# Attention outputs turned on TensorE before they are divided, in place of a way through memory, with the batch ends given a later place in the order

## The reference

```
x = x + 0.5 * ffn0(layernorm(x))       # 128 -> 512 -> 512 -> 512 -> 128, SiLU gate, two GELU layers
x = x + attn0(layernorm(x))            # linear attention, no softmax
x = x + 0.5 * ffn0(layernorm(x))
x = x + 0.5 * moe(layernorm(x))        # each batch picks 2 of 8 low-rank experts by its first position
x = x + attn1(layernorm(x))            # 16 heads of 8, rotary, causal softmax, output projection W_O
x = x + 0.5 * moe(layernorm(x))
```

```
attn = softmax(where(causal, q @ k.T * scale, -inf))     # 256 x 256
out  = attn @ v                                          # 256 x 8
y    = concat over heads(out) @ W_O.T                    # 256 x 128
```

## Time and profile before

| | |
|---|---|
| median of three runs | 768.81 us |
| lowest and highest | 764.74, 771.10 us |
| the profiled execution, whole | 767.41 us |
| its span from first to last instruction | 763.1 us |
| TensorE busy | 684.7 us, 90% |
| VectorE busy | 525.3 us, 69% |
| ScalarE busy | 502.8 us, 66% |
| GpSimd busy | 311.1 us, 41% |

### The profile page before, as it was taken

The page is one execution under the profiler, slowest core; times in us unless marked ns, Lnnn a source line. Parts: engine busy times, 40 slices in busy tenths (PEclk is TensorE's granted clock), DMA queues, the critical chain, the costliest instruction groups (busy, mean ns, idle before and its releaser), DMA issues.

```text
span 763.1 us, 14946 instructions
## 1 busy us (share of the span) xinstructions
PE 684.7 (90%) x5660; PEld 500.7 (66%) x5660; DVE 525.3 (69%) x1306; ACT 502.8 (66%) x830; POOL 311.1 (41%) x433
## 2 busy tenths in 40 slices
PE   2889999999999999999999989798879798889886
PEld 1667777778777777777787766555446355555565
DVE  3745455777657655678677768988699785979543
ACT  2767687977788867979777953346645556557541
POOL 2201121133413130224263475646668474545543
PEclk9889999999999999999999999999989898999999
DMA  9100000000110000000011123215534344332111
GB/s 294 46 1 1 0 1 1 1 0 2 38 46 0 1 1 1 0 2 1 26 58 43 43 87 107 85 47 180 169 122 149 132 152 156 102 132 99 66 57 29
DMA packets 47088, 47.29 MB, mean 62 GB/s; under 512 B 3240, under 2 KB 41128, under 8 KB 46760
## 3 DMA queue, kind: packets, MB, share of 16 engines
q1 hardware_dynamic: 47016, 46.33, 18.4%
HBM read 23.51 MB, written 22.54 MB: 60 GB/s over the span
## 4 chain that ended last, share of the span: by engine, by line
PE 47%; DVE 23%; ACT 12%; issue 6%; DMA 6%; SPq 3%; POOL 2%; POOLq 1%; DVEq 0%; ACTq 0%
PE PSA L787 16%; PE PSA L791 15%; DVE MX L1094 8%; DMA LC<-do 4%; DVE LC L1115 3%; ACT PSA L1146 3%; DVE G L1017 2%; PE PSA L804 2%; SPq L1340 2%; PE PSA L959 2%; ACT G L1142 2%; DVE RA L1087 1%; PE PSA L900 1%; ACT ah L1153 1%; ACT L1142 1%
## 5 line engine op out<-in xcount | busy, mean ns | idle before, releaser
L1240 POOL TENSOR_TENSOR RS<-VE,MHALF 128x4 f32<-128x4 f32 x48 | 49.3, 1028 | 229.7 <-DVE VE L999 229.5
L787 PE MATMUL PSA<-ah,WH 128*128 128x512 f32 x320 | 131.3, 410 | 5.7 <-DVE al L1022 3.0
L1094 DVE TENSOR_REDUCE MX<-PSA 128x6 f32<-128x768 f32 x128 | 116.9, 943 | 13.8 <-PE PSA L922 13.7
L791 PE MATMUL PSA<-al,WH 128*128 128x512 f32 x320 | 125.4, 392 | 0.0
L1146 ACT ACTIVATE PSA<-PSA,SC 128x512 f32<-128x512 f32 x128 | 84.7, 661 | 57.4 <-PE PSA L791 56.7
L1222 ACT ACTIVATE PB<-PSA 128x768 f32<-128x768 f32 x128 | 99.2, 820 | 18.3 <-PE PSA L946 18.1
L787 PE MATMUL PSA<-bh,WH 128*128 128x512 f32 x256 | 105.7, 413 | 4.0 <-DVE bl L1022 2.5
L791 PE MATMUL PSA<-bl,WH 128*128 128x512 f32 x256 | 101.2, 395 | 0.0
L1288 POOL TENSOR_SCALAR_AFFINE_SELECT PB<-PB 128x512 f32<-128x512 f32 x128 | 79.7, 636 | 43.1 <-ACT PB L1222 41.7
L1022 DVE TENSOR_TENSOR al<-PSA,ah 128x512 fp32r<-128x512 f32 x64 | 44.2, 691 | 68.8 <-ACT ah L1153 68.8
L787 PEld LDWEIGHTS PSA<-ah,WH 128*128 128x128 f32 x320 | 60.2, 188 | 22.0 <-DVE al L1022 5.2
(11 more groups left out here) (122 smaller groups left out, 1411.1 us busy)
## 6 DMA issues: line engine op xcount, KB each, us to landing
do<-OT SPq DMA_DIRECT2D x15, 512.0 KB, 6.7
KS<-dk SPq DMA_DIRECT2D x32, 192.0 KB
QS<-dq SPq DMA_DIRECT2D x32, 192.0 KB
dk<-CB SPq DMA_DIRECT2D x16, 192.0 KB, 2.3
dq<-CB SPq DMA_DIRECT2D x16, 192.0 KB, 2.4
X<-in_x SPq DMA_DIRECT2D x8, 256.0 KB, 6.9
dk<-CB SPq DMA_DIRECT2D x16, 128.0 KB, 2.2
dq<-CB SPq DMA_DIRECT2D x16, 128.0 KB, 2.4
```

Source lines behind the costliest of these rows:

```text
L787: e.matmul(o, WH[:, col:col + 128], hi, start=first, stop=False)
L791: return e.matmul(o, WH[:, col:col + 128], low, start=False, stop=last)
L1094: e.tensor_reduce(MX[:, u % 2, :, :].rearrange("p t (l g) -> p l t g", l=2)[:, :, :, g], PSA[:, b:b + 2, 0:384].rearrange("p l (t k) -> p ...
L1240: e.tensor_tensor(RS[:, i, :], VE[:, i, :], MHALF[:, :], ALU.pow).then_inc(g_rs, 1)
```

## The change

1. `ot_out`, `vl_in`, `recip`, `norm_out`, `spread` and `sel` are gone, with the memory tensor `do` and the tiles LC and SEL. Every batch, 15 too, ends in the same way.
2. `upright`, two for each batch (h = 0, 1: half of the queries): TensorE turns the four 128x128 blocks of OT for these queries into one bank, so that queries are on partitions and (head, row) on the free side; VectorE takes the reciprocal of the sixteen sums of each query (128x16, from PSUM) into RC, and multiplies the outputs by it into VQ (128x128, with the reciprocal repeated over eight).
3. `flat`, one for each batch: TensorE turns both halves of VQ back, ScalarE copies the bank to VC. Then `proj` as before; W_O is given in its plain order of rows.
4. The planner's priorities and costs: batch ends 6.6 in place of 5 (the last of all jobs), `maxima` 5.2 in place of 3.5, LEAD 28 in place of 14, QUEUED 1.0 in place of 1.5, and longer costs for `peak`, a late `stat`, and the DMAs of `reloc` and `max_out`. A `weigh` of group 0 waits in the plan until the `upright` of two batches before has been laid.

```diff
-    "rest1": [...], "reloc": [("S", 2.95, 2.95), ("D", 3.6)],
+    "rest1": [...], "reloc": [("S", 2.95, 2.95), ("D", 5.0)],
-    "pass1": [...], "peak": [("V", 0.88, 1.0)],
+    "pass1": [...], "peak": [("V", 1.7, 1.8)],
-QUEUED = 1.5
-LEAD = 14
+QUEUED = 1.0
+LEAD = 28
...
-        self.add(3.5, self.maxima(u, p1))
+        self.add(5.2, self.maxima(u, p1))
...
-        self.add(5, self.fin(u, self.last_weigh))
+        self.add(6.6, self.fin(u, self.last_weigh))
...
     def weigh(self, u, g):
+        while self.otfree[u % 2] is None:
+            yield
         b, free = yield from self.sr.get(self)
         w = self.put("weigh", u=u, g=g, b=b, emptied=free, emptied2=self.otfree[u % 2])
+        self.otfree[u % 2] = [] if g < 3 else None
...
     def fin(self, u, w):
         yield from self.until(w.done)
-        if u < NB - 1:
-            o = self.put("ot_out", u=u, c=u // 2, src=w)
-            self.otfree[u % 2] = [o]
+        while self.vqfree is None:
+            yield
+        out, vqfree, self.vqfree = [], self.vqfree, None
+        for h in range(2):
+            b, free = yield from self.sr.get(self)
+            o = self.put("upright", u=u, h=h, b=b, emptied=free, emptied2=vqfree, src=w)
+            self.sr.free[b] = [o]
+            out.append(o)
+        self.otfree[u % 2] = [o]
         while self.vcfree[u % 2] is None:
             yield
-        if u < NB - 1:
-            yield from self.until(o.done - 0.5)
-            ld = self.put("vl_in", u=u, src=o, emptied=self.vcfree[u % 2])
-            self.vcfree[u % 2] = None
-            yield from self.until(ld.done)
-            rc = self.put("recip", u=u, src=ld)
-            on = self.put("norm_out", u=u, src=rc)
-        else:
-            b, free = yield from self.sr.get(self)
-            on = self.put("spread", u=u, b=b, src=w, emptied=free, emptied2=self.vcfree[u % 2])
-            self.sr.free[b] = [on]
+        yield from self.until(o.done)
+        b, free = yield from self.sr.get(self)
+        on = self.put("flat", u=u, b=b, emptied=free, emptied2=self.vcfree[u % 2], src=o)
+        self.vqfree = self.sr.free[b] = [on]
+        self.vcfree[u % 2] = None
         yield from self.until(on.done)
         b, free = yield from self.sr.get(self)
         o = self.put("proj", c=u // 2, u=u, b=b, emptied=free, src=on)
...
# TensorE
+                elif st.name == "upright":
                     w.wait_ge(a_ot, st.src.n + 1)
+                    w.wait_ge(s_w[0], 32)
+                    emptied(w, st.emptied)
+                    for q in range(4):
+                        t = e.transpose(PSA[:, b, 128 * q:128 * q + 128], OT[u % 2][:, q, 128 * st.h:128 * st.h + 128],
+                                        IDN[:, :])
+                    t.then_inc(p_up_right, 1)
+                elif st.name == "flat":
+                    w.wait_ge(v_vq, st.src.n + 1)
+                    emptied(w, st.emptied)
+                    for h in range(2):
+                        t = e.transpose(PSA[:, b, 128 * h:128 * h + 128], VQ[:, h, :], IDN[:, :])
+                    t.then_inc(p_flat, 1)
...
# VectorE
+                elif st.name == "upright":
+                    O = bank(b).rearrange("p (m r) -> p m r", r=32)
+                    w.wait_ge(p_up_right, n + 1)
+                    e.reciprocal(RC[:, st.h, :], O[:, :, 8]).then_inc(v_rc, 1)
+                    w.wait_ge(v_rc, n + 1)
+                    for s in st.emptied2:
+                        w.wait_ge(p_flat, s.n + 1)
+                    e.tensor_tensor(VQ[:, st.h, :].rearrange("p (m r) -> p m r", r=8), O[:, :, 0:8],
+                                    RC[:, st.h, :].rearrange("p (m o) -> p m o", o=1).to_broadcast([128, NH, 8]),
+                                    ALU.mult).then_inc(v_vq, 1)
...
# ScalarE
+                elif st.name == "flat":
+                    w.wait_ge(p_flat, n + 1)
+                    for s in st.emptied2:
+                        w.wait_ge(p_proj, s.n + 1)
+                    e.activation(VC[:, u % 2, :], PSA[:, b, 0:256], ACT.Copy).then_inc(a_vc, 1)
```

More of the change, by code:

```diff
@@ L157, in put @@
         t = ready
-        for i, (eng, us, *way) in enumerate(TAKES[name]):
+        late = name + "_late" if self.dead and name + "_late" in TAKES else name
+        for i, (eng, us, *way) in enumerate(TAKES[late]):
             if eng == "D":
@@ L672, in build @@
         s_m = [sem(f"s_m{u}") for u in range(KEPT)]
-        s_dv = [sem(f"s_dv{u}") for u in range(2)]
-        s_vl = [sem(f"s_vl{u}") for u in range(2)]
-        s_out, s_sel, p_spread, v_on = sem("s_out"), sem("s_sel"), sem("p_spread"), sem("v_on")
+        s_out, p_up_right, p_flat, v_vq, a_vc = (sem(n) for n in ("s_out", "p_up_right", "p_flat", "v_vq", "a_vc"))
         p_xtf, p_up, p_hid, p_down, p_back = (sem(n) for n in ("p_xtf", "p_up", "p_hid", "p_down", "p_back"))
```

63 lines of the change are left out of this document (12 added, 51 removed), and 14 rows, old and new, of the table TAKES.

## The result

The changed kernel takes 739.85 us (median of four runs, 735.69 to 740.88), beside 767.54 us for the kernel before (median of four here, where the three above gave 768.81). The ratio is 0.9627 (95% interval 0.957 to 0.9683): 3.7% faster. The profiled execution takes 740.88 us, with a span of 739.1 us.

The account below looks back on a forecast made before the run. VectorE was taken to set the stretch from 460 us to the last `pass1`. 460.0 + 231.7 + 31.0 + 20.7 = 743.4 us of span; with 4.3 around it 747.7, plus 1.4 to the median: forecast 749 us, range 738 to 763.

Parts of the forecast that it names:

- second stretch: From 460 us to the last `pass1` reduction: VectorE's work 199.2 plus idle 32.5, 231.7 us in place of 251.0.
- third stretch: From the last `pass1` reduction to the last copy to OT: 31.0 us, against 25.7 before.
- fourth stretch: From the last copy to OT to the end, a chain of short steps: 20.7 us in place of 26.4.
- Each `upright` makes VectorE wait for four transposes: Up to the last `pass1`: 24 new waits of VectorE at 0.15 us each, +3.6 us idle.
- I take 3.6 us: Up to the last `pass1`: VectorE's waits while TensorE does 13.0 us of transposes, +3.6 us, bounds 0 and 13.0.
- The 12.1 us before the reciprocals go with the way through memory: 460 us to the last `pass1`: VectorE's idle time falls from 37.4 to 25.3 us before new waits are added.
- I book nothing for either: Up to the last `pass1`: GpSimd losing `norm_out` and SyncE's queue losing batch-end DMAs, left as an unpriced reserve.
- DMA in the way: Rival, second stage: without batch-end traffic `reloc` lands sooner and waits vanish, 741 us; chance 15%.
- The clock falls under the transposes: Rival, second stage: TensorE's clock at 0.83 in place of 0.95, a third of 31 us showing, 759 us; chance 4%.
- Half is gained: Rival, behind the last `pass1`: that stage stretches to 36.9 us, with uprights at 0.57 us, 757 us; chance 18%.
- nothing is gained: Rival, 460 us to the last `pass1`: reciprocals used idle time, so it keeps 251 us; 768 us; chance 7%.
- Slower: a batch end holds all three engines in turn: Rival, batch ends: strict order makes VectorE stand 1.3 us before each of 32 `upright`, 787 us; chance 4%.

Follow-up runs that it names:

- the old numbers: Changed kernel with the planner's costs, QUEUED 1.5, LEAD 14, maxima 3.5 and batch ends 5 of the kernel before: ratio 1.0025 to the kernel before, 765.79 us.
- the narrow kernel: Kernel before with the planner's changed numbers, VectorE's wide reciprocal cut to 8 columns (division left out), its wait for memory kept: ratio 0.9619, 739.26 us.
- the light one: Kernel before with the planner's changed numbers, wide reciprocal replaced by 8 columns of a constant, memory wait moved from VectorE to GpSimd: ratio 0.9592, 734.21 us.
- old way with new numbers: Kernel before, batch ends still through memory, with all the planner's numbers of the change: ratio 0.9818 to the kernel before, 749.46 us.
- old costs: Changed kernel with the planner's earlier costs for `reloc` (3.6), `max_out` (3.2), `peak` (0.88) and no late `stat`: ratio 0.9742 to the kernel before, 748.02 us.
- the traffic put back: Changed kernel with each batch's 512 KB out and 256 KB back, from a tile nobody else uses, so no computing engine waits: ratio 0.9653, 741.32 us.
- light kernel with old numbers: Kernel before, its order kept, wide reciprocal replaced by 8 columns of a constant, memory wait moved from VectorE to GpSimd: ratio 0.9784, 750.74 us.

## Why the prediction was right or wrong

The forecast was 9.2 us too slow. By its own terms:

| term | predicted | measured | difference |
|---|---|---|---|
| second stretch, VectorE's work | 199.2 | 202.4 | +3.2 |
| second stretch, VectorE's idle time | 32.5 | 24.9 | -7.6 |
| third stretch | 31.0 | 31.2 | +0.2 |
| fourth stretch | 20.7 | 20.6 | -0.1 |
| around the span | 4.3 | 1.8 | -2.5 |
| from the profiled execution to the median | +1.4 | -1.0 | -2.4 |

Of the first two rows, 1.3 us belong to the first stage, which ended that much sooner in this profile.

**What VectorE loses and gains: right, a little low.** "I take 0.19 us" for the reciprocal of 16 columns measured 0.248, and the multiplication 0.291 against 0.29. With 25 and 24 of them in the stretch that is 13.2 against 11.5 us, +1.7. The fixed part was mis-sized by taking a MAX8 for it. Another +1.7 is a miscount: I had two `stat` move behind the last `pass1`, and it is one. The trace has 8 of the instructions of `stat` (L992, four to a step) behind the last reduction before and 12 now (L995), two steps and three; "two `stat`" in the change's description is wrong in the same way. The rest nearly cancels: +2.5 us in L1010, 14 normalisations that are 553 ns long where they were 372, +0.7 in the reductions, and -4.3 in the three operations of `peak`, all without a change in what they do. Before and after:

```profile
L1007 DVE TENSOR_SCALAR XN<-X,MV,RS 128x128 f32<-128x128 f32 x14 | 4.7, 372 | 0.0
L1106 DVE SCALAR_TENSOR_TENSOR HM<-MX,HM 128x32 bf16<-128x32 f32 x15 | 6.6, 442 | 0.5
```

```profile
L1109 DVE SCALAR_TENSOR_TENSOR HM<-MX,HM 128x32 bf16<-128x32 f32 x15 | 4.9, 327 | 0.5
```

The upper bound of 0.81 us for a pair was far off. The reason for doubting it held: a read from PSUM kept its length. All 32 reciprocals took 239 to 259 ns and all multiplications 290 to 292, while L1109, a small operation that reads and writes SBUF alone, took between 191 and 1135:

```profile
L1109 DVE SCALAR_TENSOR_TENSOR HM<-MX,HM x16: 191/193/1135, 478.1 to 688.1; 128x32 bf16<-128x32 f32 x16
```

(ns: least, median, longest.) Eleven of the sixteen took 191 to 194 ns. The five of 503 ns and more each lie, for nearly their whole length, beside a GpSimd instruction that reads and writes SBUF; the longest:

```profile
477.87 1.30 POOL L1285 TENSOR_TENSOR RA<-RA 128x512 f32<-128x512 f32 x1 [3.74 <-DVE RA L1094]
478.08 1.14 DVE L1109 SCALAR_TENSOR_TENSOR HM<-MX,HM 128x32 bf16<-128x32 f32 x1
```

About half of the 32 reciprocals also lie beside such an instruction, and they took no longer than the others. The Trainium skill, "SBUF — State Buffer", section "Who interferes with whom", lays such stretching to a lock on ports that VectorE and GpSimd share, which a VectorE instruction with two inputs in SBUF can meet and one with at most one can't, outside certain modes. The trace agrees: L1109 has two inputs in SBUF, the reciprocal none and the multiplication one.

**"Each `upright` makes VectorE wait for four transposes" (+3.6 us) and "I take 3.6 us" for TensorE's load: the terms that were mis-sized.** Both are near nothing: 0.9 us of idle time stands before the pair, and the waits before reductions rose by 0.9. The transposes were busy 20.4 us, more than my 13.0 (I had counted 0.44 us for four, the distance to the next instruction, and the records with their overlapping ends show some 0.6), but nearly all of it went into time that was free. The bound of 0, which I had named and not taken, was nearest to what came. With the old numbers it was not: there the same steps cost 3.3 us directly, and idle time rose by 12.5 us in all although the 12.1 us before the wide reciprocals were gone.

**"The 12.1 us before the reciprocals go with the way through memory": the right number by a wrong account.** The idle time did fall by about that much. But the narrow kernel against the light one shows that such waits alone are worth some 2 to 5 us, since waits before reductions take their place; and the old way with new numbers became 14 us faster with 13.5 us of them still there. Under the old numbers the new way has none of them and idles 48.5 us; under the new numbers the old way idles 30.1 us and the new way 23.8. It takes the plan to bring the idle time down.

**The planner's numbers: the term that was missing.** I read the new order for what it moved behind the last `pass1` (5.0 us of VectorE's work, five `pass2`, two `weigh`) and, but for one `stat`, counted these rightly: 31.0 us for the third stretch measured 31.2. I booked the rest, "I book nothing for either", as a reserve. The new order by itself carries half the gain. The earlier trace rows had it in sight: a stall of 3.67 us for queries, with a planned landing of 3.6 us in the old costs. The diff raises this cost to 5.0, and a plan that reckons with late data puts other work before it; putting the old costs back gives back 9 us by the ratios. I took that for a remark on DMA traffic.

**Third stretch: right in sum, wrong in its parts.** "It cannot be shorter than that" was said of 28.2 us of ScalarE. Its groups there:

```profile
L1224 ACT ACTIVATE PB<-PSA 128x768 f32<-128x768 f32 x21 | 16.5, 816 | 0.0
L1232 ACT ACTIVATE OT<-PSA 128x256 f32<-128x256 f32 x12 | 4.5, 386 | 6.2 <-PE PSA L960 6.2
```

Twenty-one times 816 ns is 17.1 us, and the group was busy 16.5: the records of instructions overlap at their ends, within a group and still more between groups, and ScalarE was busy 24.2 us in all, idle 7.0. I had multiplied count by mean for a lower bound, which it isn't. (One `flat` fewer than the four booked stands there, 0.4 us.) Too much work and too little idle time, 2.8 us booked, cancelled.

**Fourth stretch: right step by step.** The places of the chain, from 718.45 us (end of the copies to OT):

```profile
717.78 0.67 ACT L1232 ACTIVATE OT<-PSA 128x256 f32<-128x256 f32 x2
718.98 0.60 ACT L1174 ACTIVATE XT<-PSA 128x512 f32<-128x512 f32 x1 [0.53 <-PE PSA L805]
722.15 0.38 ACT L1237 ACTIVATE VC<-PSA 128x256 f32<-128x256 f32 x1 [0.79 <-PE PSA L976]
```

```profile
719.42 0.26 DVE L1119 RECIPROCAL RC<-PSA 128x16 f32<-128x16 f32 x1 [2.51 <-PE PSA L969]
721.33 0.29 DVE L1123 TENSOR_TENSOR VQ<-PSA,RC 128x128 f32<-128x128 f32 x1
723.33 0.42 DVE L1045 TENSOR_TENSOR X<-PSA,X 128x256 f32<-128x256 f32 x1 [1.57 <-PE PSA L982]
```

I had the second division done at 3.0, the copy at 3.9 and the addition at 5.1 us; they end at 3.2, 4.1 and 5.3. VectorE waits visibly for transposes only behind the last `pass1`, 6.3 us in six waits, where little other work is left; 2.5 us of them stand here.

**The rivals.** *DMA in the way* had the nearest number, 741 us, and a cause that the runs don't bear out: the traffic put back costs about 2 us, less than the intervals. *The clock falls under the transposes* is refuted: with 124 transposes in the second stretch the granted clock is 1.00, of the level of 2.4 GHz, where it was 0.95 without them; the dips of before followed waits of TensorE, and those waits are shorter now (for queries 2.3 us in sum against 5.1). The Trainium skill, "TensorE: Matmul & The Clock Gate", section "Part 4: PE-mode transpose", says that transposes don't count as TensorE's activity in the same way. The trace shows no harm from them, but they stand in groups of two and four among products and `keep`, so it can't tell either whether they count. *Half is gained* and *nothing is gained* fell. *Slower: a batch end holds all three engines in turn* didn't happen, but its mechanism, strict order with steps in places where their data is late, is what the new way meets under the old numbers: not 38 us but 18 us given back, and just no gain.

**Around the span** I had taken the 4.3 us as fixed. They were 1.8, see the last section.

## What to carry to other kernels

When a change brings a new method and new numbers for a planner or an order, price both: run, or at least reckon, each without the other. Here the method alone gave nothing (1.0025), the numbers alone 0.9818, both together 0.9627. A wait in front of an in-order engine is worth less than its length when the engine waits for somebody else right behind it; take it away in the model and ask who is late next before booking it in full. And work laid on an engine whose idle time is filled with `keep` instructions can cost next to nothing, as it did here, as long as the plan knows its place.

## What the runs showed of the hardware that was not expected

- **Time outside the span.** The whole time less the span from first to last instruction is 4.31 us before and 4.58 us in the light kernel with old numbers (752.08 less 747.5). It is 1.71 to 1.81 us in all other kernels, among them the old way with new numbers (1.75) and the new way with old numbers (1.77). So 2.5 us of the gain lie before the first or behind the last instruction. It is there only where the old way and the old order stand together; its cause was not found.
- **The clock and the length of the first stage.** The first stage, the same up to its last instructions, ends between 459.2 and 468.3 us. In the fourteen profiles the end goes with the time that the granted clock stood at 0.50 in that stage: 6.8 us for ends at 459.2 and 460.0, 10.2 us for 460.9 to 461.6, 13.7 us for 464.7 to 466.3, 17.1 us for 467.5 to 468.3. The four runs of the kernel with old costs took 745.44, 747.11, 748.92 and 749.89 us at mean clocks of 0.989, 0.987, 0.984 and 0.983. So a stretch of one profile shouldn't be set beside that of another before both are counted from the same instruction.
- **The clock and the transposes.** 100 fp32 transposes from OT at 281 ns and 24 from VQ at 298 ns stand in a stretch with a granted clock of 1.00.
- **Short operations of VectorE.** With a source in PSUM the 128x16 reciprocal took 239 to 259 ns, beside work of GpSimd or not; L1109, on SBUF alone, took 191 to 194 ns or, beside certain instructions of GpSimd, 503 to 1135. Of the fourteen normalisations L1010, 553 ns on average, seven took 329 to 339 ns and seven 434 to 1214, the latter beside instructions of GpSimd as well.
- **A DMA's landing.** The last of four `reloc` DMAs (192 KB each) took 6.86 us from issue to landing in the place shown, nearly twice the 3.6 us of the old plan; the one of the earlier trace rows took 7.33 us.
